# Weight means in a fused attention and feed-forward block: the up weights centred by GpSimd, the output weights by ScalarE's bias

## What is computed

```python
x = x + layernorm(attn(layernorm(x), W_qkv, W_o, W_LTM, ...))
x = x + layernorm(ffn(layernorm(x), W_fc, W_proj))

# attn, for each head (16 heads of 16 features), over the tokens t
F = retention * F + coef * outer(v_t, k_t)      # k normalised over its 16 features
y_t = (W_LTM + F) @ q_t
return y @ W_o.T

# ffn
h = square(relu(x @ W_fc.T)); y = h @ W_proj.T
for _ in range(5):                              # number of spikes / 5
    reset = mem > 1; mem = 0.9 * mem + y - reset; spikes += mem > 1
```

## Time and profile before

| | |
|---|---|
| time, median of 3 runs (range) | 639.84 us (638.0 to 641.08) |
| profiled execution: time, span | 640.17 us, 638.4 us |
| VectorE busy | 534.7 us (84%) |
| TensorE busy (matmul) | 498.8 us (78%) |
| GpSimd busy | 384.3 us (60%) |
| ScalarE busy | 326.7 us (51%) |
| mean granted TensorE clock | 0.887 of full speed |

### The profile page before, as it was taken

How to read it: one execution, slowest core, us unless ns; L and a number is a source line. 1 busy time by engine, 2 the same in 40 slices (tenths; PEclk the granted TensorE clock), 3 DMA queues, 4 the chain that set the end, 5 groups by cost and what they waited for, 6 DMA issues and landing times.

```text
span 638.4 us, 7784 instructions
## 1 busy us (share of the span) xinstructions
PE 498.8 (78%) x2272; PEld 326.5 (51%) x2272; DVE 534.7 (84%) x937; ACT 326.7 (51%) x637; POOL 384.3 (60%) x184
## 2 busy tenths in 40 slices
PE   3583478449996999699979997899969995895891
PEld 1341135126673657355745665566636663473670
DVE  4799989997998999899999999999899999821001
ACT  4522123245546754656376646655567355646634
POOL 0026965785567776677677767875687667811101
PEclk9875589679897999989998999798979998988796
DMA  7364476465644575456545664567338634200000
GB/s 236 114 182 134 131 212 183 119 164 146 182 128 122 165 208 139 131 140 189 167 135 156 180 180 119 154 173 209 99 85 230 203 110 132 66 2 0 32 2 33
DMA packets 54729, 87.63 MB, mean 137 GB/s; under 512 B 5408, under 2 KB 19360, under 8 KB 54688
## 3 DMA queue, kind: packets, MB, share of 16 engines
q1 hardware_dynamic: 54112, 87.12, 48.2%
q10 hardware_dynamic: 576, 0.03, 0.1%
HBM read 78.74 MB, written 8.39 MB: 136 GB/s over the span
## 4 chain that ended last, share of the span: by engine, by line
PE 53%; issue 16%; POOL 10%; ACT 10%; DVE 10%; DMA 1%; POOLq 0%; ACTq 0%; DVEq 0%
PE p_c L346 13%; PE p_c L371 12%; PE p_a L281 7%; POOL prod L875 6%; PE p_y L324 6%; DVE state L733 5%; PE p_c L337 4%; ACT sign L547 3%; PE p_c L354 2%; PE p_a L301 2%; POOL x1t L891 2%; PE p_y L319 2%; DVE p_u L723 2%; ACT oo L468 1%; PE p_c L363 1%
## 5 line engine op out<-in xcount | busy, mean ns | idle before, releaser
L875 POOL TENSOR_TENSOR prod<-state,qf 128x1024 f32<-128x1024 f32 x128 | 302.8, 2371 | 147.5 <-DVE state L733 126.1
L733 DVE TENSOR_TENSOR_SCAN state<-ret,p_u 128x512 f32<-128x512 f32 x256 | 308.8, 1207 | 0.0
L723 DVE TENSOR_TENSOR p_u<-vrep,p_k 128x512 f32<-128x512 f32 x256 | 171.1, 674 | 2.5 <-ACT p_k L479 2.5
L346 PE MATMUL p_c<-wproj_sb,ht 128*128 128x256 f32 x512 | 116.1, 382 | 1.3 <-ACT ht L537 1.3
L371 PE MATMUL p_c<-x1t,wfc_s 128*128 128x512 f32 x384 | 99.4, 411 | 11.7 <-POOL x1t L891 10.6
L346 PEld LDWEIGHTS p_c<-wproj_sb,ht 128*128 128x128 f32 x512 | 95.7, 190 | 24.3 <-issue 9.2
L281 PE MATMUL p_a<-xt,wqkv_s 128*128 128x512 f32 x276 | 82.4, 437 | 13.9 <-POOL xt L891 5.4
L371 PEld LDWEIGHTS p_c<-x1t,wfc_s 128*128 128x128 f32 x384 | 74.4, 197 | 32.9 <-POOL x1t L891 13.7
L324 PE MATMUL p_y<-prod,summer 128*32 128x512 f32 x512 | 75.1, 661 | 8.5 <-POOL prod L875 8.5
L281 PEld LDWEIGHTS p_a<-xt,wqkv_s 128*128 128x128 f32 x276 | 53.1, 202 | 47.8 <-issue 16.3
L535 ACT ACTIVATE hr<-p_c 128x512 f32<-128x512 f32 x64 | 38.2, 597 | 36.8 <-PE p_c L371 34.9
(11 more groups left out here) (106 smaller groups left out, 481.0 us busy)
## 6 DMA issues: line engine op xcount, KB each, us to landing
vrep<-v_rows SPq DMA_DIRECT2D x256, 256.0 KB, 3.6
xa<-in_x SPq DMA_DIRECT2D x8, 512.0 KB, 5.4
v_rows<-vf SPq DMA_DIRECT2D x16, 256.0 KB, 2.0
x<-in_x SPq DMA_DIRECT2D x8, 512.0 KB, 4.7
out<-x SPq DMA_DIRECT2D x8, 512.0 KB, 3.4
ht<-in_w_fc SPq DMA_DIRECT2D x1, 1024.0 KB, 7.4
wproj_sb<-in_w_proj SPq DMA_DIRECT2D x1, 1024.0 KB, 9.9
state<-in_w_qkv SPq DMA_DIRECT2D x1, 512.0 KB, 5.5
```

The source lines that it names most:

```text
L346: last = pe.matmul(p_c[(u + 1) % 2][:, 0:D], ht[:, f, tokens(u)], wproj_sb[:, f, :], start=(f == 0), stop=(f == FT - 1))
L723: v.tensor_tensor(p_u[n % NU][:, :], vrep[:, n % NV, :], p_k[:, :], ALU.mult).then_inc(S["hebb_done"], 1)
L733: v.tensor_tensor_scan(state[:, s % NS, i, :], ret[:, r:r + 1].broadcast_to([P, L]), p_u[n % NU][:, :], 0.0, ALU.mult, ALU.add).then_inc(S ...
L875: p.tensor_tensor(prod[:, s % NZ, :, :], state[:, s % NS, :, :], qf[:, s // HS, :].unsqueeze(1).broadcast_to([P, 2, L]), ALU.mult).then_in ...
```

## The change

`centre_wide` goes from VectorE's slots 2 and 3 to GpSimd's slots 5 and 6. Since GpSimd doesn't read PSUM, ScalarE first copies the two banks of means to `hr`, in its slots 3 and 4. ScalarE's rounding copy of the up weights goes from slot 4 to slot 9, GpSimd's four low parts from slots 6 to 9 to slots 10 to 13. Of `centre_out` VectorE keeps the sum and the scaling, now by -1/D, and in slot 13 (`mean_out`); the subtraction becomes two biased copies by ScalarE in its slot 15. Two semaphores are new, `wide_copied` and `wo_mean`.

```diff
+            def centre_out():                       # ScalarE
+                act.wait_ge(S["wo_mean"], 1)
+                for half in range(HALVES):
+                    last = nc.scalar.activation(wo_sb[:, half, :], wo_sb[:, half, :], ACT.Identity,
+                                                bias=osum[:, half:half + 1])
+                last.then_inc(S["wo_centred"], 1)
...
-                    if g == 0 and s == 4:
+                    if g == 0 and s in (3, 4):
+                        copy(p_c[s - 3][:, :], hr[:, s - 3, :], "wide_mean", s - 2, "wide_copied")
+                    if g == 0 and s == 9:
                         act.wait_ge(S["wide_centred"], 2)
                         nc.scalar.copy(wfc_s[:, 0, :, :], wfc_raw).then_inc(S["wide_high"], 1)
+                    if g == 0 and s == 15: centre_out()
...
-            def centre_wide(part):                  # VectorE
-                cols = slice(part * L, (part + 1) * L)
-                dve.wait_ge(S["wide_mean"], part + 1)
-                v.tensor_tensor(wfc_raw[:, :, cols], wfc_raw[:, :, cols],
-                                p_c[part][:, :].unsqueeze(1).broadcast_to([P, KT, L]), ALU.subtract).then_inc(
-                    S["wide_centred"], 1)
-
-            def centre_out():
+            def mean_out():
                 dve.wait_ge(S["weights_in"], 48)
                 step(v.tensor_reduce(osum[:, :], wo_sb[:, :, :], AX.X, ALU.add))
-                step(v.tensor_scalar(osum[:, :], osum[:, :], 1.0 / D, None, ALU.mult))
-                for half in range(HALVES):
-                    last = v.tensor_scalar(wo_sb[:, half, :], wo_sb[:, half, :], osum[:, half:half + 1], None,
-                                           ALU.subtract)
-                last.then_inc(S["wo_centred"], 1)
+                v.tensor_scalar(osum[:, :], osum[:, :], -1.0 / D, None, ALU.mult).then_inc(S["wo_mean"], 1)
...
-                    if g == 0 and s == 1: centre_out()
-                    if g == 0 and s in (2, 3): centre_wide(s - 2)
...
+                    if g == 0 and s == 13: mean_out()
                     if after and s == 13: key_reciprocal(b, 0)
...
+            def centre_wide(part):                  # GpSimd
+                cols = slice(part * L, (part + 1) * L)
+                pool.wait_ge(S["wide_copied"], part + 1)
+                p.tensor_tensor(wfc_raw[:, :, cols], wfc_raw[:, :, cols],
+                                hr[:, part, :].unsqueeze(1).broadcast_to([P, KT, L]), ALU.subtract).then_inc(
+                    S["wide_centred"], 1)
...
-                    if g == 0 and 6 <= s < 10: low_wide((s - 6) // 2, s % 2)
+                    if g == 0 and s in (5, 6): centre_wide(s - 5)
+                    if g == 0 and 10 <= s < 14: low_wide((s - 10) // 2, s % 2)
```

More of the change, by code:

```diff
@@ L156, in build @@
             setup_ready setup_exp centred wv_high wv_low wk_high wk_low wq_high wq_low wide_high wide_low
-            ones_ready wv_mean wv_centred wkq_mean wkq_centred wide_mean wide_centred wo_centred tables_done setup_step
+            ones_ready wv_mean wv_centred wkq_mean wkq_centred wide_mean wide_copied wide_centred wo_mean wo_centred tables_done setup_step
             n1_stats n1_var n1_dev n1_step n1_done  xt_turned xt_done xt_high xt_low
```

## The result

The changed kernel takes 637.01 us (median of 13 runs, 633.62 to 640.93), the kernel before in the same comparison 640.06 us (13 runs). The ratio is 0.9949 with a 95% interval of 0.9925 to 0.9974: 3.3 us less, 1.7 to 4.8. One execution of all the runs, in e5 (787.63 us, at a granted clock of 0.63), was in a slow state and is left out.

What follows compares the result with a forecast made beforehand. VectorE, full until slot 13 of iteration 0, and the chain GpSimd, TensorE, ScalarE bound the kernel. VectorE's relief less the returning sum and the hold gave 3.25 us: 640.17 to 636.9, 636.6 against the median; range 633.0 to 639.4.

Steps and rivals of the forecast that it cites:

- The sum behind it: Reciprocal of slot 13, iteration 0, starts at 84.11 instead of 87.36, 3.25 us earlier, and all of it lasts.
- the held scaling: VectorE's two-column scaling of osum in slot 13 stands until GpSimd's product 12 ends: 1.3 us, from 82.83 to 84.11.
- VectorE's relief: Centring work of 3.65 us leaves VectorE in iteration 0, so it reaches slot 13 at 82.03 instead of 85.68.
- GpSimd's order: In iteration 0 GpSimd's subtractions take 2.31 us each, second low part of x ends at 71.1, product 12 starts at 81.75.
- The way from there to the reciprocal: From the second low part of x to the key's deviation at slot 13: 10.68 us, so ready at 81.8.
- rival (c): GpSimd's subtractions cost more than its products: gain falls from 3.5 us each, none left at 5.1 (639.8); chance 0.03.
- rival (b): Scaling in slot 13 is held past the first gap of GpSimd's queue: 637.8 at the second, to 640.2; chance 0.1.
- Rival (a): Scaling in slot 13 isn't held: the reciprocal starts at 82.83, 4.5 us earlier, giving 635.3; chance 0.3.
- (b)'s third gap: Scaling gets in only at the third gap: slot 13's reciprocal at 87.7, 0.3 later than before, 640.2, slower.
- Iteration 1 starts 3.25 us earlier on all engines: The reciprocal's whole 3.25 us reaches iteration 1 on every engine, and nothing comes back later for want of work.
- One sign of being wrong: The prediction is wrong if the gain seen at 95 us in the profile isn't there at 500.

Runs made afterwards that it cites:

- e5: Kernel before with only the output weights' half: sum and scaling in VectorE's slot 13, subtraction by ScalarE; ratio 0.9952.
- e7: As e1, but GpSimd's four low parts of the up weights stand ahead of the second low part of x again; 638.53 us, ratio 0.9950.
- e10: Kernel before, unchanged, profiled a second time; stage to slot 13 54.96 us, no ratio given.
- e12: Kernel before with ten unused matmuls added in TensorE's idle time of iteration 0; ratio 0.9971.
- e8: e1 with eight small unused VectorE instructions added beside running GpSimd products; timed once, 644.96 us, serves for its trace alone.
- e2: Changed kernel with the two-column scaling of osum made by two one-column instructions, still in slot 13; 633.63 us, ratio 0.9876.
- e11: Changed kernel, unchanged, second look; 637.67 us, ratio 0.9937 to the kernel before.
- e1: Changed kernel with the sum and scaling of osum moved from VectorE's slot 13 into the setup; 636.21 us, ratio 0.9901.
- e3: Changed kernel with the sum and scaling of osum back in VectorE's slot 1, ScalarE still subtracting; ratio 0.99.
- e9: Changed kernel with GpSimd's four low parts in one row behind product 12 and VectorE's sum over the output weights made twice; ratio 0.9905.

## Why the prediction held, point by point

**The size** came out: 636.6 forecast, 637.01 measured. The sum behind it did not. It gives 3.25 us to the reciprocal of slot 13, and the stages show 1.6 to 2.1 of them, because the held scaling cost twice its term. The timed 3.3 us (1.7 to 4.8) hold that and perhaps more, which comes from no term of the sum. So far as they go beyond 2.1, that the forecast's number was met is luck.

**VectorE's relief** held to 0.1 us. Slot 13 was reached at 81.74; 82.03 was worked out, and the setup was 0.17 shorter.

**GpSimd's order** held: second low part of x at 70.92 (71.1), product 12 at 81.58 (81.75), subtractions at 2.34 and 2.36 us (2.31 start to start). The rival (c) is out. e7 shows the step on which this rests, that the low parts of the weights go behind that of x.

**The way from there to the reciprocal** was taken as 10.68 us, at the clock of before. It took 8.5 (70.92 to 79.45). It didn't matter for the changed kernel, since VectorE came later than either. But the other side of the sum is touched: the removed wait of 1.68 us isn't a constant of the kernel before (e10: 1.21; e12: none with TensorE busy). I had weighed the clock only as noise in later iterations; it belonged into the term itself.

**The held scaling** is the step that was right in kind and mis-sized. Held: yes, and by what the rows suggested (e8). Price: 1.3 us forecast, to the end of product 12; measured 2.6 (2.77 less the 0.17 that it takes), to the end of the low part. That is rival (b) at its second gap, of which the prediction said 637.8. The reciprocal came at 85.11, not 84.11: 2.25 us earlier than before, not 3.25. Rival (a) is out. (b)'s third gap, the slower case, didn't come.

**"Iteration 1 starts 3.25 us earlier on all engines", and nothing comes back**: the way held, the size was 2.3: GpSimd's first product of iteration 1 began 2.27 us earlier (99.79; 102.06 before), as much as the reciprocal. But later stages vary with TensorE's clock, and by more than the change is worth. Iteration 1 took 65.16 and 66.62 us in two looks at the changed kernel, and 63.8 in four of the variants. All of that is VectorE's wait at slot 13 of iteration 1, from 2.1 us in those four to 4.9; here e2 and e11:

```profile
146.60 0.35 DVE L711 RECIPROCAL krd<-kdev 128x32 f32<-128x32 f32 x1 [2.11 <-ACT kdev L497]
```

```profile
151.54 0.35 DVE L709 RECIPROCAL krd<-kdev 128x32 f32<-128x32 f32 x1 [4.89 <-ACT kdev L497]
```

Ahead of it, from the projection of v on, the granted clock was 0.88 in e2 and 0.67 in e11; the projection of k took 1.54 us and 2.76. So it is the clock; whether its early rise in those four belongs to their timing or to chance is open.

One sign of being wrong, the gain of 95 us not there at 500, can't be read from single profiles. From the first normalised key to the reciprocal of iteration 6 the changed kernel was 6.2 us shorter in the first looks and 0.8 longer in the second ones, which had two dips against one. That the gain lasts rests on the timed ratios. Why these give 3.3 us (1.7 to 4.8) and in the second comparison 4.0 (1.9 to 6.2), where the stage shows 1.6 to 2.1, is open; the lower ends of the intervals lie within that.

## What to carry to other kernels

Before a small VectorE instruction moves to "a free slot", look at what GpSimd does there. Here two columns of a scaling cost 2.6 us beside a full GpSimd and 0.2 as two instructions of one column, or where GpSimd was idle (e1) or at the end of its product (e3). A version of the change with single columns (e2) gains about twice as much, by the stage and by the ratio. And work moved to the engine on the path costs nothing only if as much is moved behind the instruction that the path hangs on.

## What the runs showed of the hardware that I had not expected

- A VectorE tensor_scalar or copy as short as two or three columns stands still beside a GpSimd tensor_tensor until that ends: 1.95 to 1.98 us in place of 0.14 to 0.2 (e8). One column, a reciprocal and a reduction don't (0.14 to 0.15 us).
- At the joint of two GpSimd instructions the held one got in twice (e9, e8's two-input instruction) and was passed over once, at the same place in two executions (2.77 and 2.76 us). I found no rule.
- TensorE's granted clock rises at different places in executions of one kernel: a pair of matmuls in the same place took 1.91 and 1.43 us in two looks at before (e10). The setup took 31.4 to 36.3 us in kernels whose setup is the same or 0.8 us of VectorE's work apart, and ten matmuls that nothing uses, in TensorE's idle time, were worth 1.9 us (0.6 to 3.1; e12).
